# Context rows normalised by ScalarE from a scale and a shift column, in place of VectorE

## The reference, cut to what matters

```
xn = (ctx - mean(ctx)) / sqrt(var(ctx) + 1e-5) * g_x + b_x    # 16 x 512 rows of 512
ln = the same for the latents with g_l, b_l
k, v = concat(xn, ln) @ w_kv ; q = ln @ w_q                    # 8 heads of 64
x = x + norm(softmax(q k^T / 8) v @ w_out)
```

## Time and profile before

| | |
|---|---|
| median of three runs | 1062.05 us (1061.95 to 1063.06) |
| profiled execution | 1062.28 us, of which span 1060.5 us |
| TensorE busy | 995.0 us (94%), 6468 matmuls |
| VectorE busy | 792.1 us (75%) |
| ScalarE busy | 424.8 us (40%) |
| GpSimd busy | 146.4 us (14%) |
| prologue (latents) | 0 to about 72 us |
| batches 0 to 15 | about 85 to 672 us, 75.2 us a pair of batches |
| self attention, feed-forward | the rest |

### The profile page before, as it was taken

The page is one execution under the profiler, slowest core; times in us unless marked ns, Lnnn a source line. Parts: engine busy times, 40 slices in busy tenths (PEclk is TensorE's granted clock), DMA queues, the critical chain, the costliest instruction groups (busy, mean ns, idle before and its releaser), DMA issues.

```text
span 1060.5 us, 16689 instructions
## 1 busy us (share of the span) xinstructions
PE 995.0 (94%) x6468; PEld 781.6 (74%) x6468; DVE 792.1 (75%) x1736; ACT 424.8 (40%) x747; POOL 146.4 (14%) x163
## 2 busy tenths in 40 slices
PE   5999999999999999999999999899999879999996
PEld 4887888788787877787787888545555658888884
DVE  7356787997987988988888964266477578989983
ACT  4534465356446545543654553222232312222211
POOL 1310011210210212112111110032132000000000
PEclk9999999999999999999999999999999989999998
DMA  6955342441443244234423332070000350000000
GB/s 240 271 155 166 78 125 63 120 130 48 124 128 101 76 118 135 77 95 115 123 68 107 108 100 89 15 274 1 1 2 29 131 218 11 11 11 11 11 11 20
DMA packets 72446, 98.50 MB, mean 93 GB/s; under 512 B 38320, under 2 KB 47152, under 8 KB 70064
## 3 DMA queue, kind: packets, MB, share of 16 engines
q1 hardware_dynamic: 65008, 72.80, 23.0%
q0 software_dynamic: 7360, 24.65, 7.4%
HBM read 67.54 MB, written 29.88 MB: 92 GB/s over the span
## 4 chain that ended last, share of the span: by engine, by line
PE 73%; DVE 17%; ACT 5%; issue 3%; DMA 1%; SPq 0%; POOL 0%; DVEq 0%; ACTq 0%
PE ps_banks L146 15%; PE ps_banks L148 15%; PE ps_banks L147 15%; PE ps_banks L533 10%; PE ps_banks L412 7%; PE ps_banks L507 2%; PE ps_banks L653 2%; PE ps_banks L652 2%; PE ps_banks L654 2%; DVE sb_b_stats L743 1%; DVE sb_wq_big L916 1%; DVE sb_w_q L924 1%; DVE sb_ctx L756 1%; DVE sb_kT_lo L782 1%; ACT sb_zT_hi L1301 1%
## 5 line engine op out<-in xcount | busy, mean ns | idle before, releaser
L146 PE MATMUL ps_banks<-sb_zT_hi,sb_wkv_hi 128*128 128x512 f32 x256 | 106.2, 415 | 3.7 <-DVE sb_kT_lo L782 3.7
L146 PE MATMUL ps_banks<-sb_wkv_hi,sb_zT_hi 128*128 128x512 f32 x256 | 104.9, 410 | 0.0
L148 PE MATMUL ps_banks<-sb_wkv_hi,sb_zT_lo 128*128 128x512 f32 x256 | 100.5, 392 | 0.0
L148 PE MATMUL ps_banks<-sb_zT_hi,sb_wkv_lo 128*128 128x512 f32 x256 | 100.4, 392 | 0.0
L147 PE MATMUL ps_banks<-sb_zT_lo,sb_wkv_hi 128*128 128x512 f32 x256 | 99.9, 390 | 0.0
L147 PE MATMUL ps_banks<-sb_wkv_lo,sb_zT_hi 128*128 128x512 f32 x256 | 99.8, 390 | 0.0
L1257 ACT ACTIVATE sb_kT_hi<-ps_banks 128x512 fp32r<-128x512 f32 x64 | 38.1, 596 | 148.1 <-PE ps_banks L148 148.1
L146 PE MATMUL ps_banks<-sb_wgu,sb_z_hi 128*128 128x512 f32 (+1 forms) x192 | 74.7, 389 | 1.0 <-DVE sb_z_lo L782 1.0
L147 PE MATMUL ps_banks<-sb_wgu,sb_z_hi 128*128 128x512 f32 (+1 forms) x192 | 73.0, 380 | 0.0
L148 PE MATMUL ps_banks<-sb_wgu,sb_z_lo 128*128 128x512 f32 (+1 forms) x192 | 73.0, 380 | 0.0
L782 DVE TENSOR_TENSOR sb_zT_lo<-sb_zfull,sb_zT_hi 128x512 fp32r<-128x512 f32 x64 | 44.1, 690 | 28.5 <-ACT sb_zT_hi L1301 28.3
(11 more groups left out here) (229 smaller groups left out, 2440.5 us busy)
## 6 DMA issues: line engine op xcount, KB each, us to landing
sb_ctx<-in_ctx SPq DMA_DIRECT2D x16, 1024.0 KB, 5.9
sb_wgu<-scratch_wgu SPq DMA_DIRECT2D x8, 1024.0 KB, 9.1
scratch_wgu<-sb_w_hi POOLq DMA_DIRECT2D x22, 256.0 KB, 2.8
scratch_wgu<-sb_w_lo POOLq DMA_DIRECT2D x22, 256.0 KB, 3.2
sb_wdn<-scratch_wdn SPq DMA_DIRECT2D x2, 2816.0 KB, 12.9
scratch_q<-sb_a_qk POOLq DMA_DIRECT2D x8, 512.0 KB, 6.2
sb_qpack<-scratch_q SPq DMA_DIRECT2D x32, 128.0 KB, 5.8
sb_wgu<-scratch_wgu SPq DMA_DIRECT2D x4, 768.0 KB, 13.5
```

What stands on the lines that cost most here:

```text
L146: e.matmul(o, wh, xh, start=i == 0, stop=False)
L148: m = e.matmul(o, wl, xh, start=False, stop=i == n - 1)
```

## The change

`normalise` stops after the statistics and computes one more small column set: shift = -mean x rstd, a single VectorE instruction on 128x4 elements, which raises a new semaphore `z_shift_ready`. The four passes over the rows are gone from VectorE. In their place stands `normal_z` on ScalarE: row = Identity(rstd x row + shift), in place, with rstd as scale column and shift as bias column. For batch 0 the four are queued in the prologue behind `hi_of_latent_key(1, 3)` and ahead of `hi_of_z(0, 0)`; for the others two each in slots 2 and 3, ahead of that slot's `hi_of_k`. A tile of 16 bytes a partition is added.

```diff
+        shift_b = sb(ctx, "b_shift", [P, CS])
...
-        z_normed, z_split = sem("z_normed"), sem("z_split")
+        z_normed, z_split, z_shift_ready = sem("z_normed"), sem("z_split"), sem("z_shift_ready")
...
                 nth = finish_stats(0, CS, small_b)
                 yield
-                for i in range(CS):
-                    normal(src[i], src[i], i, small_b, nth, z_normed)
-                    yield
+                on.wait_ge(rstd_ready, nth)
+                e.scalar_tensor_tensor(out=shift_b[:, :], in0=small_b[1][:, :, 0], scalar=-1.0, in1=small_b[3][:, :],
+                                       op0=ALU.mult, op1=ALU.mult).then_inc(z_shift_ready)
+                yield
...
-                    advance(norm, (2, 3, 2, 9)[slot] if slot < 4 else 0)
+                    advance(norm, (2, 3, 9)[slot] if slot < 3 else 0)
...
+            def normal_z(b, k):
+
+                on.wait_ge(z_shift_ready, b + 1)
+                row = ctx_in[b % 2][:, k, :]
+                e.activation(row, row, ACT.Identity, bias=shift_b[:, k:k + 1], scale=small_b[3][:, k:k + 1]).then_inc(z_normed)
+
...
                 hi_of_latent_key(1, n)
+            for k in range(CS):
+                normal_z(0, k)
             for n in range(C):
                 hi_of_z(0, n)
...
                         copy_y(t_new)
+                    if nxt and slot in (2, 3):
+                        normal_z(b + 1, 2 * slot - 4)
+                        normal_z(b + 1, 2 * slot - 3)
                     if cur and slot < 4:
                         hi_of_k(b, slot)
```

## The result

The changed kernel takes 1066.22 us (median of 11 runs, 1063.98 to 1067.29), and the kernel before, on the same chip, 1063.18 us (11 runs, 1061.95 to 1064.11). The ratio is 1.0026, with a 95% interval of 1.0017 to 1.0034: slower by 1.8 to 3.6 us. Measured again with five rounds it was 1.0009 [1.0000, 1.0017], 1065.65 against 1063.93 us. The forecast was 1063.2 us, range 1060.2 to 1065.4. Both medians of after lie above the range. Yet nearly every single step of the forecast is found in the profile; what follows is about how that goes together.

What follows compares the result with a forecast made beforehand. TensorE was taken as the bound, busy for 995.0 of 1060.5 us. +3.65 - 1.2 - 2.65 - 0.16 = -0.4 us, +1.2 with the clock's loss, on a base of 1062.05 us gave 1063.2 us; range 1060.2 to 1065.4.

Steps and rivals of the forecast that it cites:

- The base: Whole kernel: the summed difference was put onto 1062.05 us, the median before; the profiled execution was 0.2 us above it.
- The stop at the start: Prologue, batch 0's first context transposes: TensorE waits for four ScalarE passes queued behind the last latent key, a 3.65 us loss.
- Batch 0, slots 3 and 4: TensorE's 1.16 us wait for the second pair of normalisations goes, as ScalarE has the passes ready earlier: 1.2 us gained.
- Odd batches: Odd batches 3 to 11: weight block 0.75 us earlier, ScalarE's chain late next; 0.53 us gained each, 2.65 us in all.
- Batch 13 and even batches: Batch 13: the same ScalarE chain ends at 580.90 against 581.06, 0.16 us gained; even batches and batch 1: nothing.
- The clock: Behind the stop in the prologue: TensorE's granted clock falls for one short stretch of 3.4 us, costing 1.6 us; chance 0.47.
- The sum: Whole kernel: -0.4 us without the clock's loss, +1.2 us with it, giving 1063.2 us.
- A held clock: Rival, behind the prologue's stop: the clock doesn't fall, 1061.7 us; chance 0.22.
- ScalarE late and no gain in the odd batches: Rival: ScalarE's chain takes 0.53 us more, so odd batches gain nothing, 1067.2 us; chance 0.07, shared with worthless VectorE relief.
- Cheap passes: Rival, all ScalarE passes: columns cost less, a pass counts 0.52 us; 1060.7 us with clock loss, 1059.1 without; chance 0.10.
- VectorE's relief worthless: Rival: VectorE's 30 us don't come off; start, batch 0 and clock remain, 1066.1 us; chance 0.07, shared with late ScalarE.
- The long stretch of low clock: Rival, behind the prologue's stop: 6.8 us of low clock, costing 2.7 us, 1064.4 us, up to 1065.1; chance 0.14.

Runs made afterwards that it cites:

- after_tiles_in_place: The changed kernel with 32 bytes of padding behind the new tile, putting later tiles at their old offset within 64 bytes: 1066.36 us, 1.0021 of before.
- batch0_on_vector: The changed kernel with batch 0's passes back on VectorE, the other 15 batches on ScalarE: 1058.41 us, 0.9959 of before.
- batch0_on_scalar_only: The kernel before with only batch 0's passes moved to ScalarE, in the prologue: 1067.80 us, 1.0037 of before; repeated, 1070.08 us, 1.0047.

## Why the prediction was wrong, point by point

Two steps failed: the base that the sum was put onto, and the clock term, which was too small and was looked for at one place only.

- **The base.** The sum was put onto 1062.05 us, the median of three runs. Medians of before from 11 to 35 runs were 1063.18 to 1063.93 us, the mean of 118 is 1063.7. So 1.1 us (the same session's median) to 1.9 us of the 3.0 us (1066.22 - 1063.2) by which the forecast missed were in the base before the change came in. With the session's own base and the measured terms (+1.3 us, see the sum) about 1.7 us of the miss remain. The traces show where runs differ: TensorE was already 1.9 us late at 50 us in after, 0.2 us in after_tiles_in_place, with the same instructions up to there (its first projection starts at 15.88 us against 14.42 in before, and the clock is 0.66 from 17 to 22 us). The clock of whole runs differs too: the 53 runs of before at 0.994 or more take 1063.0 us in the mean, the 41 at 0.990 or less 1064.6. The profiled execution of before was a quick one as well, so that "0.2 above the median" confirmed nothing. The range held the unknown costs of the change and nothing for this scatter.
- **The stop at the start: right.** Forecast 3.65 us, found 3.65, with TensorE idle for 3.50. Pass price 0.80 us (forecast 0.81), four in 2.91 us (0.70 from start to start). The Trainium skill ("ScalarE: Activation LUTs", section What ACT_TABLE_LOAD costs) gives 0.80 us by its formula, and with one column element and both columns 0.37 us; the traces agree, 803 ns and 375 ns.
- **Batch 0, slots 3 and 4: right**, 1.27 us for 1.2.
- **Odd batches: right**, 0.57 us for 0.53 each, with the new wait of 0.34 us for the passes. That ScalarE's chain is late next was shown by moving the sign behind the passes. What VectorE's relief allows was put at 0.75 to 0.9 us; it is about 1.05 us, as the cheap passes and the moved sign show.
- **Batch 13 and even batches: right**, 0.2 and 0.
- **The clock: right in kind, too small in size.** Forecast 1.6 us from the short stretch; 2.0 us at the stop in the mean of five traces, since the long stretch came in two of the five and not in one of four, as 0.14 against 0.47 supposed. That is 0.4 us of the error. The sum had no term for low clock anywhere else; in whole runs the changed kernel has 7 us more of it than before and 2.7 us left over beside the places.
- **The sum.** 3.65 - 1.27 - 2.85 - 0.2 + 2.0 = +1.3 us with the measured terms, against +1.2 forecast. The changed kernel's 22 runs lie 2.0 ± 0.3 us above before. Of the 0.7 us between them low clock away from the stop could be most: 7 us more of it at 0.35 are 2.5 us, an estimate from the table, and the stop has 2.0 of these. No trace shows the rest at a place, and so it isn't attributed. The two measurements of the same pair (1.0026 and 1.0009) differ by 1.8 us themselves, more than their errors allow, so the true effect is at the edge of what I called measurable, at about +0.2%, and the forecast of "no change" with 0.70 was nearer to an even bet with "slower".
- **Rivals.** A held clock: refuted by every trace with the whole stop. ScalarE late and no gain in the odd batches: refuted, they gain. Cheap passes: refuted, 0.80 us. VectorE's relief worthless: refuted by batch0_on_vector. The long stretch of low clock was real, in two traces of five.

## What to carry to other kernels

Moving work to an idler engine is priced by the place it gets in that engine's queue: here the same passes gave -0.4% without batch 0's, -0.24% spread among the key copies, and +0.1 to +0.26% behind them. When a freed engine's work starts to pay, look at the order of the newly loaded engine at that spot: what nobody awaits yet (the sign) goes behind what is awaited (the passes), and that raised the gain of an odd batch from 0.57 to 1.05 us and that of the kernel from 4.5 to 6.5 us (traces, 50 us to stage D). And a forecast of a few tenths of a per cent needs a base of many runs: three runs can be off by more than the whole effect. Where the clock has two levels, compare the time at the lower one over whole runs, not only at the changed place.

## What the runs showed of the hardware

- A single stop of TensorE of 3.5 us inside an otherwise full stream cost 1.5 to 2.8 us on top of itself, at the lower clock level, in every one of five traces; matmuls without use in the stop avoided it (0.06 us or less in two traces). The Trainium skill ("TensorE: Matmul & The Clock Gate", section The HAM clock gate) says that the number of slow matmuls differs from run to run for one kernel; the traces agree: one kernel, batch0_on_scalar_only and its repetition, lost 1.53 and 2.51 us behind the same 3.50 us wait.
- A stop of 1.92 us cost 1.65 us in one trace and a stop of 2.09 us nothing in another; 1.79 us cost nothing, 2.76 us cost 1.63 us. Near 2 us the length of the stop alone doesn't tell.
- The time at the lower clock level differs between runs of one kernel (mean granted clock 0.987 to 0.995 in before) and between kernels away from the changed place (0.89, 0.94 and 1.00 from 830 to 860 us in three traces). What the places left over of a kernel's time went with it, about 0.35 us for each us at the lower level, over 15 rows.
- A tile of 16 bytes a partition ahead of all later ones, which moves their addresses, did nothing (1.0003 [0.9992, 1.0013]).
